# The order of projection and output products within an attention step of a sandwich transformer block

## What is computed

```
q = (x @ wq.T + bq).reshape(B, S, H, hd)      # k and v alike; B 2, S 2048, H 16, hd 64
scores = einsum('bqhd,bkhd->bhqk', q, k) * inv_sqrt_hd
scores = where(causal, -inf, scores)
probs = softmax(scores, axis=-1)
attn = einsum('bhqk,bkhd->bqhd', probs, v).reshape(B, S, D)
return attn @ wo.T + bo
...
x = x + layernorm(attention(layernorm(x)))
x = x + layernorm(ffn(layernorm(x)))
```

## Time and profile before

| | us |
|---|---|
| median of 3 runs | 2405.65 |
| lowest and highest run | 2402.87 and 2406.46 |
| span of the profiled execution | 2400.4 |
| PE busy in it | 2271.6 |
| DVE / ACT / POOL busy in it | 1675.7 / 1741.4 / 1633.9 |

### The profile page before, as it was taken

One profiled execution on the slowest core, in us unless ns is written; L12 is line 12 of the kernel. 1 busy time (PEld: TensorE's weight loads), 2 busy tenths in 40 slices (PEclk: granted clock), 3 DMA queues, 4 the chain that ended last, 5 costly groups with the idle time before them and its releaser, 6 DMA issues. The chain is left out here.

```text
span 2400.4 us, 70752 instructions
## 1 busy us (share of the span) xinstructions
PE 2271.6 (95%) x28666; PEld 1448.5 (60%) x28666; DVE 1675.7 (70%) x4148; ACT 1741.4 (73%) x2380; POOL 1633.9 (68%) x1291
## 2 busy tenths in 40 slices
PE   6999999999999998899999999999999679999996
PEld 4566667575757655557575757575766445455453
DVE  8487777777777766566666666666676846777777
ACT  6577777877777766677777777777787846666665
POOL 3588888888888876678788888888898822222221
PEclk9999999999999999999999999999999889999998
DMA  8699999999999999999999999999999986656662
GB/s 244 124 196 202 194 211 207 196 203 204 209 197 197 208 200 198 198 200 193 174 195 181 189 183 187 185 184 185 182 192 195 232 169 155 165 153 174 149 168 79
DMA packets 1414420, 447.44 MB, mean 186 GB/s; under 512 B 1391664, under 2 KB 1392064, under 8 KB 1414096
## 3 DMA queue, kind: packets, MB, share of 16 engines
q1 hardware_dynamic: 1414096, 442.92, 99.7%
HBM read 67.95 MB, written 41.94 MB: 46 GB/s over the span
## 5 line engine op out<-in xcount | busy, mean ns | idle before, releaser
L1051 POOL TENSOR_TENSOR hl<-probs,hl 128x1024 f16<-128x1024 f32 x544 | 1166.6, 2151 | 350.2 <-ACT hl L903 348.1
L896 ACT ACTIVATE probs<-s_ps,exp_bias 128x1024 f32<-128x1024 f32 (+7 forms) x768 | 633.3, 854 | 316.5 <-DVE exp_bias L730 309.7
L725 DVE TENSOR_REDUCE neg_max<-s_ps 128x1 f32<-128x1024 f32 (+7 forms) x768 | 675.8, 904 | 169.2 <-PE s_ps L526 169.1
L903 ACT ACTIVATE hl<-probs 128x1024 f16<-128x1024 f32 x544 | 575.0, 1057 | 90.2 <-DMA pt<-hl 74.1
L549 PE MATMUL o_ps<-v,pt 128*128 128x65 f16 x4352 | 431.1, 193 | 50.2 <-DMA pt<-hl 43.8
L549 PEld LDWEIGHTS o_ps<-v,pt 128*128 128x128 f16 x4352 | 400.5, 96 | 79.3 <-DMA pt<-hl 36.9
L526 PE MATMUL s_ps<-nat 64*128 64x512 f16 (+3 forms) x3840 | 410.1, 351 | 25.9 <-ACT probs L896 22.4
L550 PE MATMUL o_ps<-v,pt 128*128 128x65 f16 x4352 | 431.4, 194 | 0.0
L551 PE MATMUL o_ps<-v,pt 128*128 128x65 f16 x4352 | 430.2, 192 | 0.0
L550 PEld LDWEIGHTS o_ps<-v,pt 128*128 128x128 f16 x4352 | 399.8, 97 | 19.1
L551 PEld LDWEIGHTS o_ps<-v,pt 128*128 128x128 f16 x4352 | 400.3, 98 | 0.0
(11 more groups left out here) (185 smaller groups left out, 3580.9 us busy)
## 6 DMA issues: line engine op xcount, KB each, us to landing
w_raw<-in_w_pairs SPq DMA_DIRECT2D x48, 576.0 KB, 4.8
o_scratch<-o_hl SPq DMA_DIRECT2D x128, 128.0 KB, 2.6
out<-result SPq DMA_DIRECT2D x31, 512.0 KB, 3.1
x_in<-in_x SPq DMA_DIRECT2D x27, 512.0 KB, 4.9
pt<-hl SPq DMA_TRANSPOSE x544, 5.2
xn_scratch<-xn SPq DMA_DIRECT2D x16, 512.0 KB, 3.8
xn<-in_x SPq DMA_DIRECT2D x11, 512.0 KB, 3.8
x_in_c<-in_x SPq DMA_DIRECT2D x10, 512.0 KB, 3.9
```

The source lines that it names most:

```text
L725: nc.vector.tensor_reduce(neg_max[:, step.round, acc, h:h + 1], s_ps[(n + h) % S_RING][:, first:end], AX_X, ALU.max, negate=True).then_inc ...
L896: last = nc.scalar.activation(probs_of(n)[:, cols], s_ps[n % S_RING][:, cols], ACT.Exp, bias=exp_bias[:, step.round, acc, h:h + 1], scale= ...
L903: nc.scalar.activation(hl_of(n, 0), probs_of(n), ACT.Copy).then_inc(p_hi_done, 1)
L1051: nc.gpsimd.tensor_tensor(hl_of(n, 1), probs_of(n), hl_of(n, 0), ALU.subtract).then_inc(p_lo_done, 1)
```

## The change

In `body` of PE's block the two calls of `times_v` are taken apart. Head 0's output products now come right behind the scores, then the projection's slice, then head 1's output products.

```
@@ def body(p, kind), PE's block
                     step = step_of(p, i, kind)
                     if step:
                         scores(*step)
+                    times_v(p, i, 0)
                     for u, part, count in UNIT_AT[kind][i:i + 1]:
                         atoms = ATOMS[order_of(units_of(p))[u][0]] // count
                         project(units_of(p), u, part * atoms, (part + 1) * atoms)
-                    for h in range(2):
-                        times_v(p, i, h)
+                    times_v(p, i, 1)
```

## The result

The changed kernel takes 2416.59 us (median of 7 runs, 2414.3 to 2419.8), the kernel before in the same sessions 2406.11 us (7 runs). The ratio is 1.0041 with a 95% interval of 1.0027 to 1.0055: **slower by about 10 us**. The forecast was 2414, in a range of 2402 to 2427.

What follows compares the result with a forecast made beforehand. PE bounds the kernel, except where transposes set the pace (840 to 1060 us, from 1740 us). 8.6 + 8.2 + 3.8 = 20.6, less 10 and 2: +8.6 on 2400.4, 2409.0; plus 5.25 gives 2414 us, range 2402 to 2427.

Steps and rivals of the forecast that it cites:

- Reads that are late anyway: Opening steps up to 841 us: DVE's read of the last round comes after PE wants it, 8.6 us.
- Late units: Units end 0.72 us later; where a norm piece stands between unit and read, DVE's read is later too: 8.2 us.
- 12 x 0.72 - 0.47: Twelve rounds from 188 to 841 us each delay the read 0.72 us; one was 0.47 us early: 8.2 us.
- the 25 to 35 foretold: Sign: before 840 us, PE's head 0 product waits for DVE's read some 25 to 35 times.
- the 10 to 18 foretold: Sign: those waits of PE for DVE's read before 840 us come to 10 to 18 us.
- Head 0's transposes: Before 840 us, five transposes of head 0's probabilities land after PE now wants them, 3.8 us together.
- What is absorbed: Before 840 us, a later PE finds its 12.1 us of waits for exponentials partly over: 10 us taken back.
- The border: Output product to projection row, 259 steps: costed at nothing; as rival, 0.10 us each, +26 us (2440), chance 0.04.
- The stretch from 840 to 1060 us: Output products wait for transposes there anyway; new waits replace old ones, 0 in sum.
- The ring: Head 1's transpose slot comes free sooner: -2 us by the last transpose-bound stretch; as rival, -11 us (2395), chance 0.10.

Runs made afterwards that it cites:

- Experiment 1: Head 0's product ahead of the projection only at steps that open a round, against the kernel before: ratio 1.0025, +6.0 us.
- experiment 5: The changed kernel with DVE's norm piece moved ahead of the unit's evacuation, against the kernel before: ratio 1.0001, +0.2 us.
- experiment 4: The new order only in pairs 7 to 15, which have no layer norm pieces, against the kernel before: ratio 1.0001, +0.2 us.
- `late_pairs`: The kernel of experiment 4, with the order of before up to the start of pair 7: ratio 1.0001 against the kernel before.
- Experiments 2 and 7: Head 0's product ahead of the projection only at steps not opening a round: ratio 1.0003; the same with norm piece before the unit's evacuation: 0.9999.
- experiment 6: The kernel before, PE's order kept, with DVE's norm piece moved ahead of the unit's evacuation: ratio 0.9999 against the kernel before.

## Why the prediction was right

The mechanism stands: PE waits for reads of the last round that the projection slice had covered, the cost comes before 840 us, and nothing from 1060 to 1740 us. That the number came so close is in part luck, as three of its terms show.

- **Reads that are late anyway, 8.6 us.** Right. Experiment 1, which has them and no late units ahead of them, shows 10.0 us of waits in 15 places.
- **Late units, 8.2 us.** Right in mechanism and in the sum: over the same rounds, up to 860 us, the changed kernel has 18.1 us of waits for the read, 8.1 us more than experiment 1. Moving the norm piece out from between unit and read (experiment 5) takes the loss away. But the step "12 x 0.72 - 0.47" is wrong round by round, and the sum came out by luck. Against experiment 1, six of the twelve rounds wait at most 0.07 us longer, since the norm piece got shorter as the unit got later; the other six wait 0.7 to 1.1 us longer, 4.8 us in all twelve. Another 3.1 us come from six rounds that the prediction did not count: DVE had idled at most 0.05 us ahead of the unit there, and with the later unit it idles 0.4 to 0.8 us. The waits for the read were 20 up to 840 us, fewer than the 25 to 35 foretold, at 17.2 us within the 10 to 18 foretold.
- **Head 0's transposes, 3.8 us.** Over-sized: 0.6 us. The five places were found against landings of the trace of before; a PE that late reads have pushed back comes to them later. That this is the reason was not tried.
- **What is absorbed, 10 of 12.1 us.** Over-sized: waits for exponentials fell by 6.7 us, from 12.1 to 5.4.
- **The border, 0.** Right: 0.03 us in the trace after, and 0.2 us for 140 steps in experiment 4. The Trainium skill's rule on weight loads of the same row group ("TensorE: Matmul & The Clock Gate", section The mechanism), by which the border would have cost about 28 us as an estimate, does not hold for these matmuls. The same section of the Trainium skill excepts loads into a background weight buffer, which the prediction left out; no trace here shows whether these loads are such ones.
- **The stretch from 840 to 1060 us, 0 in sum.** Right as far as the traces can tell. Against the trace of before, the changed kernel is 13.2 us behind at the start of pair 6 and 13.7 us at the start of pair 9; against that of `late_pairs`, 10.2 and 9.1 us.
- **The ring, -2 us.** Not there. The slot waits shrank from 50 us to 6, as foretold, and SP then waited for POOL's low halves, 102.1 us in place of 30.4. Experiments 2 and 7 show no gain.

By the terms: 17.2 + 0.6 - 6.7 = 11.1 us up to 840 us, where the prediction had 20.6 - 10 = 10.6; with the ring's -2, which was not there, it forecast 8.6 in all, beside about 10 measured. Two terms that were too large offset each other, transposes by 3.2 us and absorbed waits by 3.3, so the sum was closer than its parts.

What stays open: why the five transposes of head 0 cost so little, and how much of the waits for exponentials a later PE finds over, which was taken as 10 of 12.1 us with little reason. The last 4 us between 11.1 and the 15.9 us of the two spans are mostly the low trace of before: against the span of `late_pairs`, 2405.5 us, the changed kernel's is 10.8 us longer. And the 8 reads that stay late in experiment 5 were not removed alone.

## What to carry to other kernels

When an instruction is moved ahead of a block of work on the engine that bounds the kernel, ask what that block had been hiding: list every semaphore the moved one waits for, and lay each release against its new place, step by step, not on average. Here 22 of 122 releases were late at the new place, and they made about half of the waits. The other half came by way of the work that was pushed back: it ended 0.72 us later, and an in-order queue carried that lateness past a filler piece to the release, wherever the piece itself did not get shorter by as much. Filler on a second engine belongs into that engine's own waits, ahead of the awaited instruction, and not between it and what the bounding engine wants next. Where the bounding engine does not want the release early, this is worth nothing (experiment 6).

## What was not expected of the hardware

The same norm instruction on DVE took very different times from one execution to the next: line 664 lasted 0.85 us at 235.86 us above, 1.24 us in experiment 5 and 1.58 us in the trace before, each time the same piece of the same tile. Line 669, of the same size, lasted 3.15 us at 249.68 us.

The traces show what sets these times: the POOL instruction that is under way when DVE's begins. At 235.86 us it is this one, of the changed kernel, which ends at 236.16:

```profile
235.00 1.16 POOL L1056 TENSOR_TENSOR nat<-full,nat 128x512 f16<-128x512 f32 x1
```

DVE's line 664 ends at 236.71, 0.55 us after it. In the trace of before the POOL instruction ends at 234.41 and DVE's at 234.96, 0.55 us after it again, though DVE's had begun 1.03 us ahead of POOL's end and not 0.30 us. I laid all 171 executions of line 664 and all 165 of line 669 up to 860 us, in all eleven traces, against POOL. With no POOL instruction under way they last 0.80 and 1.21 us. With one under way they end 0.55 us (line 664) and 1.08 us (line 669) after its end, to 0.04 us, or last 0.80 and 1.21 us if that is more. Three of the 336 last longer; in each of them the next POOL instruction began within 0.03 us of DVE's start. Line 703, which reads PSUM and not SBUF, lasts 0.73 to 0.75 us in all 631 executions, whatever POOL does. That DVE waits for POOL is thus a reading of all the traces; no run moved POOL's work to try it.

This is why a late unit was free in half of the twelve rounds: a norm piece that begins later under the same POOL instruction ends when it would have ended anyway.
